# Moving three small jobs of a state-space main loop off VectorE, with new places for all small steps

## The chip, the cores and the metric

The kernel runs on one core of one Trainium2 chip. Its measure is the device time of one execution in microseconds (us), lower is better. Engines are named as in the profile: PE (TensorE matmul; PEld is its weight load), DVE (VectorE), ACT (ScalarE), POOL (GpSimd) and SP (SyncE, which here issues DMAs).

## The reference, cut to what matters

64 images are cut into 196 patches each and embedded into 192 channels; with a class token that gives 197 tokens per image. Then comes one block with a selective state-space layer, and a routed feed-forward layer with 8 experts. Cut to what the change touches:

```
def _forward(x, W_in, conv_w, conv_b, W_x, W_dt, b_dt, A_log, D, W_out, gamma, beta):
    xz = x @ W_in
    x_inner, z = jnp.split(xz, 2, axis=-1)
    x_conv = lax.conv_general_dilated(x_inner, conv_w, ...) + conv_b
    x_conv = silu(x_conv)
    BC = x_conv @ W_x
    Bm, Cm = jnp.split(BC, 2, axis=-1)
    delta = jax.nn.softplus(x_conv @ W_dt + b_dt)
    A = -jnp.exp(A_log)
    def step(h, inp):
        x_t, d_t, B_t, C_t = inp
        A_disc = jnp.exp(d_t[:, :, None] * A)
        h = A_disc * h + (d_t * x_t)[:, :, None] * B_t[:, None, :]
        y_t = jnp.einsum('bds,bs->bd', h, C_t)
        return (h, y_t)
    ...
    y = y * silu(z)
    out = y @ W_out
    mu = jnp.mean(out, axis=-1, keepdims=True)
    var = jnp.mean(jnp.square(out - mu), axis=-1, keepdims=True)
    return (out - mu) * lax.rsqrt(var + 1e-05) * gamma + beta
h = h + _L0_attn_ref(_layernorm(h, axis=-1), ...)
h = h + _L0_ffn_ref(_layernorm(h, axis=-1), ...)
```

The first layer norm is over the embedded tokens, the second ("out" norm) is the one inside the state-space layer, the third is in front of the router.

## The kernel before, in words

Images are worked on in 32 pairs; a pair is 2 x 197 = 394 columns. One body of the main loop holds several pairs at different depths: pair i is scanned, pair i+1 gets its convolution, B, C and softplus, pair i+2 its embedding and first norm, and pair i-1 its output product and its norms. Bodies run from i = -2 to 33, so that there are 32 bodies with a scan.

The scan of a pair is 12 units `u` (3 channel blocks x 4 groups of states), each in two halves, 24 half units `k`. For one unit PE spreads a row group of B over the partitions (`spread_b`, into one PSUM bank), DVE multiplies it with delta*u (`bx`, L1302), ACT makes the decays by an exponential with a scale from `neg_a` (`decays`, L661, two instructions for each half unit, into one of only two PSUM buffers), DVE scans each half unit (`scan`, L1311), POOL multiplies the states with C (`times_c`, L489) and PE sums the states (`state_sum`, L970). DVE takes the sum of a channel block times the gate into `y` (`take_y`, L1324).

Around that skeleton stand the small steps, each written at a fixed unit or half unit of the `body` function of its engine, with waits on semaphores. There is no scheduler: every engine runs its rows in the order written, and a row that waits holds all behind it. `decays(n, k)` waits until scan k-2 has ended, since the two decay buffers alternate. `kbank(K, odd)` gives the small products two PSUM banks in turn, and the numbers `K_OF`, `OUT`, `TOKS`, `FT`, `BT`, `CS`, `ROUTE` say which product has which bank; the waits in PE's `body` follow that order.

The steps that the change moves from DVE are three. `out_stats` computes the mean and variance of the output product of pair i-1 (BATCH_NORM_STATS2 L1285, BATCH_NORM_AGGREGATE L1290), after which POOL makes a reciprocal deviation and a bias (`rstd`, L478 to L483) and ACT applies both (`normalise`, L668). `softplus_t` rounds 1 + exp(-|v|) and takes the 1 away again (L1340), which POOL uses for the lost part of the logarithm. `last_bc` makes the third bf16 part of the product that holds B and C (L1317); three bf16 parts together carry an fp32 value through a bf16 matmul.

Behind the loop the tokens get their router probabilities, ranks and slots. Most columns, `FIRST` (the first 31 pairs), are treated inside the last bodies; those of the last pair, `LAST`, after them. The steps are `shift`, an exponential on ACT, `weigh` (L1360 to L1364), `choose` (L1369 to L1374), `rank` on PE and `ranks` on DVE (L1383 to L1397).

## Time and profile before

| | before |
|---|---|
| median of 3 runs | 3121.68 us (3120.38 to 3123.74) |
| the profiled execution's own time | 3125.05 us |
| its span from first to last instruction | 3123.3 us |
| mean granted clock of PE, as a share | 0.899 |
| busy over the span: PE, DVE, ACT, POOL | 2551.4, 2516.7, 1970.8, 2153.0 us |

The span is split into a start (to the first `bx` at 121.94 us), the 32 scan bodies (to 2473.55 us, the end of the last scan), the router work and the expert layer. In a row of the profile the times are microseconds from the start of the span; an idle time in brackets is the wait of the engine just before the row, with what ended it.

### The profile page before, as it was taken

Reading aid. Unit: us, or ns where it says so; the run is one execution under the profiler, and the core shown is the slowest. Engines: PE = TensorE matmul, PEld = TensorE weight load, DVE = VectorE, ACT = ScalarE, POOL = GpSimd, SP = SyncE. Lnnn points to the kernel's source line nnn. Section 1 sums busy time; section 2 is a strip of 40 time slices with the busy share of each in tenths; the row PEclk is TensorE's granted clock in tenths of the full one; section 3 lists DMA queues with packets and bytes.
Section 4 is the critical chain, followed back from the end, with each engine's and each line's share of the span. In section 5 each row is a group of like instructions: output and inputs, shape, how many; then the busy total and the mean of one; then the engine's idle time right before and its main releaser. Section 6 shows DMA issues by size and latency. Waiting matters only on the chain.

```text
span 3123.3 us, 38093 instructions
## 1 busy us (share of the span) xinstructions
PE 2551.4 (82%) x12714; PEld 1570.2 (50%) x12714; DVE 2516.7 (81%) x2800; ACT 1970.8 (63%) x3883; POOL 2153.0 (69%) x1291
## 2 busy tenths in 40 slices
PE   5688888878888888888888878788886567999997
PEld 3344444444444444444444444444442256888886
DVE  1499999999999999999999999999999875322222
ACT  0577777777777777777777777777676464333332
POOL 0378788877888887778888887788787613544442
PEclk8899899988899999989999998888898679999999
DMA  3344444444554544444444444454453023666652
GB/s 95 93 94 101 102 101 105 115 115 108 114 118 116 115 107 102 102 102 101 102 101 101 102 117 106 114 114 114 108 118 91 8 74 111 220 215 206 210 188 99
DMA packets 165466, 361.10 MB, mean 116 GB/s; under 512 B 18353, under 2 KB 89593, under 8 KB 157848
## 3 DMA queue, kind: packets, MB, share of 16 engines
q1 hardware_dynamic: 152504, 329.59, 42.0%
q0 software_dynamic: 12768, 29.08, 2.9%
q8 instruction: 103, 1.69, 0.2%
q14 instruction: 91, 0.75, 0.1%
HBM read 293.86 MB, written 69.30 MB: 116 GB/s over the span
## 4 chain that ended last, share of the span: by engine, by line
PE 38%; DVE 33%; issue 13%; ACT 13%; POOL 1%; DMA 1%; SPq 0%; DVEq 0%; POOLq 0%; ACTq 0%
DVE arena L1311 15%; DVE arena L1302 11%; PE banks L1218 7%; PE banks L1197 5%; PE banks L941 4%; PE banks L904 4%; PE banks L1205 2%; PE banks L970 2%; PE banks L932 2%; PE banks L923 2%; ACT banks L661 2%; ACT arena L668 1%; DVE arena L1340 1%; DVE arena L1285 1%; ACT L741 1%
## 5 line engine op out<-in xcount | busy, mean ns | idle before, releaser
L489 POOL TENSOR_TENSOR arena<-arena 128x1576 f32<-128x1576 f32 x384 | 1244.2, 3255 | 286.7 <-DVE arena L1311 286.7
L1311 DVE TENSOR_TENSOR_SCAN arena<-banks,arena 128x788 f32<-128x788 f32 x768 | 1359.8, 1789 | 58.7 <-ACT banks L661 20.5
L661 ACT ACTIVATE banks<-arena,neg_a 128x392 f32<-128x392 f32 x1536 | 842.3, 581 | 421.8 <-DVE arena L1311 415.2
L1302 DVE TENSOR_TENSOR arena<-arena,banks 128x1576 f32<-128x1576 f32 x384 | 681.3, 1774 | 29.4 <-DMA arena<-delta_du_scratch 16.8
L970 PE MATMUL banks<-arena,gather_q 128*32 128x394 f32 x3072 | 380.2, 571 | 0.2 <-POOL arena L489 0.2
L1513 DVE TENSOR_TENSOR arena<-banks,arena 128x384 f32<-128x384 f32 x57 | 31.8, 558 | 346.3 <-PE banks L1218 346.3
L904 PE MATMUL banks<-wtok,arena 128*99 128x192 f32 x1536 | 264.3, 329 | 49.1 <-ACT arena L728 44.3
L923 PE MATMUL banks<-arena,v_lo 128*128 128x394 f32 x768 | 291.5, 523 | 2.5 <-ACT arena L698 1.1
L904 PEld LDWEIGHTS banks<-wtok,arena 128*99 128x99 f32 x1536 | 249.0, 167 | 81.2 <-ACT arena L728 65.6
L624 POOL DMA_INDIRECT out_tokens<-arena x114 | 114.7, 1006 | 245.0 <-DVE arena L1528 225.2
L668 ACT ACTIVATE arena<-arena 99x192 f32<-99x192 f32 x384 | 178.8, 536 | 124.2 <-POOL arena L483 119.6
L1218 PE MATMUL banks<-arena 128*128 128x192 f32 x1368 | 232.5, 326 | 0.7 <-DVE arena L1513 0.7
L1218 PEld LDWEIGHTS banks<-arena 128*128 128x128 f32 x1368 | 221.5, 190 | 1.4 <-DVE arena L1513 1.0
L923 PEld LDWEIGHTS banks<-arena,v_lo 128*128 128x128 f32 x768 | 143.3, 196 | 153.8 <-issue 59.2
L914 PE MATMUL banks<-ident,arena 99*128 99x99 f32 x128 | 43.6, 366 | 216.1 <-ACT arena L698 127.3
L941 PE MATMUL banks<-arena,wdt 128*128 128x394 f32 x576 | 211.1, 512 | 5.7 <-ACT arena L737 4.9
L862 ACT ACTIVATE arena<-banks 128x256 f32<-128x256 f32 x57 | 22.0, 385 | 304.1 <-PE banks L1184 304.1
L616 POOL DMA_INDIRECT arena<-rows_scratch,arena x114 | 118.0, 1035 | 122.2 <-DVE arena L1505 87.8
L955 PE MATMUL banks<-arena,pick 128*128 128x394 bf16 x384 | 142.5, 371 | 71.5 <-DVE arena L1302 71.4
L941 PEld LDWEIGHTS banks<-arena,wdt 128*128 128x128 f32 x576 | 105.5, 192 | 113.7 <-issue 29.3
L1197 PE MATMUL banks<-arena 128*128 128x256 f32 x684 | 159.1, 381 | 4.0 <-ACT arena L864 2.4
L970 PEld LDWEIGHTS banks<-arena,gather_q 128*32 128x32 f32 x3072 | 64.2, 115 | 189.1 <-issue 184.8
(217 smaller groups left out, 4237.8 us busy)
## 6 DMA issues: line engine op xcount, KB each, us to landing
arena<-delta_du_scratch SPq DMA_DIRECT2D x384, 394.0 KB, 11.2
arena<-in_w_pack SPq DMA_DIRECT2D x57, 1155.0 KB, 5.2
delta_du_scratch<-arena SPq DMA_DIRECT2D x96, 394.0 KB, 3.3
arena<-in_x SPq DMA_DIRECT2D x32, 1176.0 KB, 15.8
rows_scratch<-arena SPq DMA_DIRECT2D x32, 297.0 KB
rows_scratch<-arena SPq DMA_DIRECT2D x32, 294.0 KB
arena<-in_b SPq DMA_DIRECT2D x57, 96.0 KB, 5.2
arena<-in_conv_w SPq DMA_DIRECT2D x1, 2304.0 KB, 9.1
```

What stands on the lines that cost most here:

```text
L489: pool.tensor_tensor(v[:, :, :], v[:, :, :], c_rep[r][:, u % NG].unsqueeze(1).to_broadcast([P, NQ, N2]), ALU.mult).then_inc(s_mulp, 1)
L661: ins = act.activation(o, d, ACT.Exp, scale=neg_a[:, c:c + 1])
L668: ins = act.activation(dst(c), src(c), ACT.Identity, scale=rs[:, c:c + 1], bias=nb[:, c:c + 1])
L904: mm = pe.matmul(v[0:H0, f * DIM:(f + 1) * DIM], patches[:, c, b, f * HSTEP:f * HSTEP + H0], wtok[:, c, :], start=(c == 0), stop=(c == KP ...
L923: pe.matmul(v[:, 0:N2], v_lo[:, k, c], t_lo[:, :, k:k + L], start=(k == 0), stop=False)
L941: mm = pe.matmul(v[:, 0:N2], wdt[:, k, c], xz[r][:, k, :], start=(k == 0), stop=(k == MB - 1))
L955: pe.matmul(ps_b[:, 0:N2], pick[:, u % NG, :], bc3[r], start=True, stop=True).then_inc(s_bb, 1)
L970: mm = pe.matmul(ps_y[q * 32:(q + 1) * 32, 0:N2], gather_q[:, :], hb[u % BUFS][:, q, :], start=False, stop=(g == NG - 1), skip_group_check ...
L1197: pe.matmul(hidden_part(k, f), wp[g][:, f * P:(f + 1) * P], x[:, 0, :], start=(f not in (2, 3, 5)), stop=False, skip_group_check=True)
L1218: mm = pe.matmul(ps_out[:, f * DIM:(f + 1) * DIM], hid[k % 2][:, c, f * P:(f + 1) * P], w2[:, c, :], start=(c == 0), stop=(c == KF - 1))
L1302: dve.tensor_tensor(hb[u % BUFS][:, :, :], rep[m][:, :, 1, :], ps_b[:, 0:N2].unsqueeze(1).to_broadcast([P, NQ, N2]), ALU.mult).then_inc(s_ ...
L1311: dve.tensor_tensor_scan(v, decay[k % 2], v, 0.0, ALU.mult, ALU.add).then_inc(s_scan, 1)
```

## The change

Three jobs leave DVE, and all small steps of all four engines get new units, half units and banks.

The output norm: the columns of `wout` are centred once in the start (the mean of each row is taken away), so that the product has a mean of zero; ACT then squares the product with `Square` and an accumulated sum (`out_squares`), POOL makes the reciprocal deviation from it in two instructions instead of four (`rstd_out`), and ACT applies it as a scale alone. The softplus rounding becomes two ACT instructions, +1 and -1 (`softplus_up`, `softplus_t`). The third part of B and C becomes a subtraction on POOL (`last_bc`) and a copy to bf16 on ACT (`third_bc`).

The places: the third norm's application, the back transposes and the router of a pair run one body later than before (pair i-2 instead of i-1), two of the three convolutions and the copy of the gate's `Silu` run one body earlier, two of the four C spreads one body later, and at the end `choose` and `ranks` of `FIRST` stand behind the loop instead of inside it.

```diff
-        K_OF = (0, 1, 2, 6, 5, 7, 8, 9, 14, 13)
-        MADE = (1, 2, 3, 5, 4, 6, 7, 8, 10, 9)
-        TAKEN = (1, 3, 2, 5, 4, 6, 7, 8, 10, 9)
-        OUT, TOKS, FT = (3, 4), (10, 11), (16, 18)
-        BT, CS, ROUTE = (19, 20), (12, 15, 17, 21), 22
+        K_OF = (21, 1, 20, 4, 5, 9, 8, 13, 16, 14)
+        MADE = (2, 3, 1, 4, 5, 7, 6, 8, 10, 9)
+        TAKEN = (2, 3, 1, 4, 5, 7, 6, 8, 10, 9)
+        OUT, TOKS, FT = (6, 7), (11, 12), (17, 18)
+        BT, CS, ROUTE = (3, 10), (19, 22, 0, 2), 15
...
+            def rstd_out(n):
+                need(pool, s_onorm, n)
+                pool.wait_ge(s_sq2, n + 1)
+                pool.tensor_scalar(var2[:, :], sq2[:, :], 1.0 / DIM, EPS, ALU.mult, ALU.add).then_inc(s_var2, 1)
+                pool.wait_ge(s_var2, n + 1)
+                pool.tensor_tensor(rs2[:, :], var2[:, :], small[0:H0, 0, :], ALU.pow).then_inc(s_rs2, 1)
...
+            def last_bc(n, r):
+                pool.wait_ge(s_bcmid, n + 1)
+                pool.tensor_tensor(bcf, bcf, bc3[r], ALU.subtract).then_inc(s_bclast, 1)
...
+            def out_squares(n, r):
+                act.wait_ge(s_oev, 2 * (n + 1))
...
+                for c in range(4):
+                    ins = act.activation(rows[r][:, c, DIM:2 * DIM], ob[:, c, :], ACT.Square, accum_out=sq2[:, c:c + 1])
+                ins.then_inc(s_sq2, 1)
+
             def out_norm(n):
-                normalise(n, lambda c: ob[:, c, :], lambda c: ob[:, c, :], rs2, nb2, s_rs2, s_onorm, range(4))
+                act.wait_ge(s_rs2, n + 1)
+                for c in range(4):
+                    ins = act.activation(ob[:, c, :], ob[:, c, :], ACT.Copy, scale=rs2[:, c:c + 1])
+                ins.then_inc(s_onorm, 1)
...
+            def third_bc(n, r):
+                act.wait_ge(s_bclast, n + 1)
+                act.activation(bc3[r][P - 2 * NS:P], bcf[P - 2 * NS:P], ACT.Copy).then_inc(s_bc3, 1)
...
+            def softplus_up(n):
+                act.wait_ge(s_spe, n + 1)
+                need(act, s_ddu, DDU * n)
+                act.activation(delta[:, :, :], spe[:, :, :], ACT.Identity, bias=1.0).then_inc(s_spu, 1)
+
+            def softplus_t(n):
+                act.wait_ge(s_spu, n + 1)
+                act.activation(delta[:, :, :], delta[:, :, :], ACT.Identity, bias=-1.0).then_inc(s_spt, 1)
...
-            def last_bc(n, r):
-
-                v = slice(P - 2 * NS, P)
-                dve.wait_ge(s_bcmid, n + 1)
-                dve.tensor_tensor(bc3[r][v], bcf[v], bc3[r][v], ALU.subtract).then_inc(s_bc3, 1)
-
...
-            def out_stats(n):
-                stats(n, lambda c: ob[:, c, :], st2, mv2, s_oev, 2 * (n + 1), s_rs2, s_st2, s_mv2)
-
...
-            def softplus_t(n):
-                dve.wait_ge(s_spe, n + 1)
-                need(dve, s_ddu, DDU * n)
-                dve.tensor_scalar(delta[:, :, :], spe[:, :, :], 1.0, -1.0, ALU.add, ALU.add).then_inc(s_spt, 1)
...
-                    if -1 in on and k == 10:
-                        out_stats(i - 1)
-                        if i == PAIRS:
-                            choose(FIRST)
...
-                    if 1 in on and k == 15:
-                        last_bc(i + 1, o)
-                    if 1 in on and k == 15:
-                        softplus_t(i + 1)
...
+                    if -2 in on and k == 19:
+                        take_logits(i - 2, r)
+                        if i == PAIRS:
+                            shift(FIRST)
+                        if i == PAIRS + 1:
+                            weigh(FIRST, 1)
...
             for i in range(-2, PAIRS + 2):
                 body(i, i % 2, range(-i, PAIRS - i))
+            choose(FIRST)
+            ranks(FIRST, 1)
```

DVE, half units 10 to 15 of one middle body. L1302 is `bx`, L1311 the scan (listed under this name by the compiler), L1285 and L1290 the statistics, L1317 `last_bc`, L1340 `softplus_t`, L1277 the embedding, L1324 `take_y`. Before:

```order
L1311 SCALAR_TENSOR_TENSOR arena<-banks,arena 128x788
L1285 BN_STATS arena<-arena 99x6 x4
L1290 BN_AGGR arena<-arena 99x2 x4
L1311 SCALAR_TENSOR_TENSOR arena<-banks,arena 128x788
L1302 TENSOR_TENSOR arena<-arena,banks 128x1576
L1311 SCALAR_TENSOR_TENSOR arena<-banks,arena 128x788 x2
L1302 TENSOR_TENSOR arena<-arena,banks 128x1576
L1311 SCALAR_TENSOR_TENSOR arena<-banks,arena 128x788
L1324 TENSOR_TENSOR arena<-arena,banks 128x394
L1311 SCALAR_TENSOR_TENSOR arena<-banks,arena 128x788
L1317 TENSOR_TENSOR arena<-arena 32x394
L1340 TENSOR_SCALAR arena<-arena 128x3x394
```

The same stretch in the changed kernel, half units 10 to 16, where L1386 is `bx`, L1395 the scan, L1402 `take_y` and L1361 the embedding:

```order
L1386 TENSOR_TENSOR arena<-arena,banks 128x1576
L1395 SCALAR_TENSOR_TENSOR arena<-banks,arena 128x788 x2
L1386 TENSOR_TENSOR arena<-arena,banks 128x1576
L1395 SCALAR_TENSOR_TENSOR arena<-banks,arena 128x788 x2
L1402 TENSOR_TENSOR arena<-arena,banks 128x394
L1386 TENSOR_TENSOR arena<-arena,banks 128x1576
L1395 SCALAR_TENSOR_TENSOR arena<-banks,arena 128x788
L1361 TENSOR_TENSOR arena<-banks,tok_bias 99x384
L1395 SCALAR_TENSOR_TENSOR arena<-banks,arena 128x788
L1386 TENSOR_TENSOR arena<-arena,banks 128x1576
L1395 SCALAR_TENSOR_TENSOR arena<-banks,arena 128x788
L1361 TENSOR_TENSOR arena<-banks,tok_bias 99x384
```

The eight rows of the output statistics and the rows L1317 and L1340 are gone; `take_y` and the embedding stand a half unit earlier.

ACT, half units 9 and 10. Before, with L741 the `Silu` of z, L737 that of x and L680 the copy of the output product:

```order
L661 ACTIVATE banks<-arena,neg_a 128x2x196 x2
L741 ACT_TABLE_LOAD
L741 ACTIVATE arena<-arena 128x1182
L737 ACTIVATE arena<-arena 128x1182
L680 ACTIVATE arena<-banks 99x384
L661 ACT_TABLE_LOAD
L661 ACTIVATE banks<-arena,neg_a 128x2x196 x2
L680 ACTIVATE arena<-banks 99x384
```

The changed kernel, half units 9 to 13, with L680 the decays, L699 the copies of the output product, L708 the squares, L754/L755 the softplus reads, L780 the exponential, L785 and L789 +1 and -1, L801/L802 a copied back transpose:

```order
L699 ACTIVATE arena<-banks 99x384 x2
L708 ACTIVATE arena<-arena 99x192 x4
L680 ACTIVATE banks<-arena,neg_a 128x2x196 x4
L754 ACTIVATE arena<-banks,bdt 128x394
L755 ACTIVATE arena<-banks,bdt 128x394
L680 ACTIVATE banks<-arena,neg_a 128x2x196 x2
L754 ACTIVATE arena<-banks,bdt 128x394
L755 ACTIVATE arena<-banks,bdt 128x394
L780 ACTIVATE arena<-arena 128x1182
L680 ACTIVATE banks<-arena,neg_a 128x2x196 x2
L785 ACTIVATE arena<-arena 128x3x394
```

The two `Silu` instructions, which shared one pair of table loads, now stand apart (L776 at the end of a body, L772 in half unit 5), each with a load ahead of it and one behind it:

```order
L776 ACT_TABLE_LOAD
L776 ACTIVATE arena<-arena 128x1182
L680 ACT_TABLE_LOAD
L680 ACTIVATE banks<-arena,neg_a 128x2x196 x2
```

```order
L772 ACT_TABLE_LOAD
L772 ACTIVATE arena<-arena 128x1182
L734 ACTIVATE arena<-banks 128x394
L801 ACTIVATE arena<-banks 128x198
L802 ACTIVATE arena<-banks 64x198
L680 ACT_TABLE_LOAD
L680 ACTIVATE banks<-arena,neg_a 128x2x196 x2
```

So a body has six table loads on ACT, where it had four.

## Rows read from the trace of the kernel before

**Rows 1.** Busy time of each engine in a middle stretch.

```profile
core 0: us, PE busy (x) PEld busy (x) DVE busy (x) ACT busy (x) POOL busy (x), PEclk, DMA share, GB/s
1500.00:2000.00 500.00, 411.81 (x1989) 222.71 (x1991) 482.65 (x465) 360.41 (x675) 404.35 (x216) 0.90 0.48 111
```

**Rows 2.** What DVE waited for, 500 to 2300 us: total, times, longest.

```profile
DVE arena L1311 <- ACT banks L661: 16.8, 25, 1.2
DVE arena L1302 <- PE banks L955: 7.8, 8, 2.0
```

**Rows 3.** Timeline of DVE: start, duration, row, count, idle before.

```profile
165.81 0.77 DVE L1317 TENSOR_TENSOR arena<-arena 32x394 bf16<-32x394 f32 x1
...
1530.91 1.77 DVE L1302 TENSOR_TENSOR arena<-arena,banks 128x1576 f32<-128x1576 f32 x1
...
1536.19 1.77 DVE L1302 TENSOR_TENSOR arena<-arena,banks 128x1576 f32<-128x1576 f32 x1
...
1551.28 1.11 DVE L1285 BATCH_NORM_STATS2 arena<-arena 99x6 f32<-99x192 f32 x4
1552.85 0.38 DVE L1290 BATCH_NORM_AGGREGATE arena<-arena 99x2 f32<-99x6 f32 x4 [0.46 <-DVE arena L1285]
1553.14 1.76 DVE L1311 TENSOR_TENSOR_SCAN arena<-banks,arena 128x788 f32<-128x788 f32 x1
...
1565.97 0.74 DVE L1317 TENSOR_TENSOR arena<-arena 32x394 bf16<-32x394 f32 x1
...
1568.05 0.55 DVE L1277 TENSOR_TENSOR arena<-banks,tok_bias 99x384 f32<-99x384 f32 x1
```

**Rows 4.** Groups of ACT by form, 1500 to 2260 us.

```profile
L661 ACT ACTIVATE banks<-arena,neg_a 128x392 f32<-128x392 f32 x495 | 271.5, 581 | 125.6 <-DVE arena L1311 124.8
L668 ACT ACTIVATE arena<-arena 99x192 f32<-99x192 f32 x128 | 59.6, 536 | 20.8 <-POOL arena L483 19.3
L661 ACT ACT_TABLE_LOAD x21 | 26.9, 1283 | 0.4
...
L737 ACT ACTIVATE arena<-arena 128x1182 f32<-128x1182 f32 x10 | 11.8, 1176 | 0.0
```

**Rows 5.** Timeline of ACT around one table load.

```profile
1542.06 1.10 ACT L661 ACTIVATE banks<-arena,neg_a 128x392 f32<-128x392 f32 x2 [0.49 <-DVE arena L1311]
1543.18 1.28 ACT L741 ACT_TABLE_LOAD   x1
1544.47 1.19 ACT L741 ACTIVATE arena<-arena 128x1182 f32<-128x1182 f32 x1
```

**Rows 6.** Groups of POOL by form, 1500 to 2260 us.

```profile
L489 POOL TENSOR_TENSOR arena<-arena 128x1576 f32<-128x1576 f32 x123 | 398.6, 3257 | 80.9 <-DVE arena L1311 80.9
...
L495 POOL TENSOR_TENSOR arena<-arena 128x394 f32<-128x394 f32 x10 | 9.3, 934 | 10.2 <-ACT arena L718 10.2
```

**Rows 7.** Timeline of PE: one softplus product early, and one in the middle.

```profile
148.43 4.02 PE L941 MATMUL banks<-arena,wdt 128*128 128x394 f32 x6 [1.13 <-ACT arena L737]
...
1547.17 2.25 PE L941 MATMUL banks<-arena,wdt 128*128 128x394 f32 x6
```

**Rows 8.** Timeline of DVE, POOL and PE behind the last scan.

```profile
2471.76 1.79 DVE L1311 TENSOR_TENSOR_SCAN arena<-banks,arena 128x788 f32<-128x788 f32 x1
...
2482.46 0.57 DVE L1324 TENSOR_TENSOR arena<-arena,banks 128x394 f32<-128x394 f32 x1 [0.61 <-PE banks L970]
...
2518.97 0.17 DVE L1445 TENSOR_SCALAR arena<-arena 99x8 int32<-99x8 f32 x1
...
2467.94 12.86 POOL L489 TENSOR_TENSOR arena<-arena 128x1576 f32<-128x1576 f32 x4
...
2510.40 0.48 PE L999 MATMUL banks<-sww_hi,arena 128*99 128x8 f32 x2
```

**Rows 9.** Busy time of each engine in two stretches: `weigh`, and `choose` to `ranks`.

```profile
2482.93:2486.52 3.59, 3.35 (x11) 3.08 (x12) 3.51 (x5) 0.00 (x0) 0.00 (x0) 0.50 0.00 0
2491.24:2512.35 21.11, 10.45 (x32) 5.54 (x32) 15.38 (x29) 4.71 (x12) 15.66 (x27) 0.64 0.10 30
```

More of the change, by code:

```diff
@@ L594, in body @@
                             router_consts()
-                    if 0 in on and u == 5:
+                    if 0 in on and u == 2:
                         fill_rows(i, r)
-                    if -1 in on and u == 8:
+                    if -1 in on and u == 7:
                         apply_gamma(i - 1)
+                    if 2 in on and u == 7:
+                        rstd(i + 2, 1)
                     if -1 in on and u == 8:
@@ new lines, in body @@
+                    if 0 in on and k == 2:
+                        copy_c(i, r, r, 2)
+                    if -2 in on and k == 2:
+                        row_norm(i - 2, r)
+                        if i == PAIRS + 1:
+                            router_exp(FIRST, 1)
+                    if 1 in on and k == 4:
+                        copy_product(i + 1, o, r, 1)
+                    if 1 in on and k == 5:
+                        silu_x(i + 1, o)
+                    if 0 in on and k == 5:
+                        copy_c(i, r, r, 3)
@@ L1114, in body @@
-                    if -1 in on and u == 10:
+                        if 2 in on:
+                            pe.wait_ge(s_trf_copied, 2 * (i + 2) + 1)
+                        else:
+                            pe.wait_ge(s_lg, i - 2 + 1)
+                        spread_c(i + 1, o, r, 0)
+                    if 2 in on and u == 10:
+                        pe.wait_ge(s_trf_copied, 2 * (i + 2) + 2)
+                        conv(i + 2, r, r, 2)
+                    if 2 in on and u == 11:
                         if 1 in on:
-                            pe.wait_ge(s_cc, NG * (i + 1) + 3)
+                            pe.wait_ge(s_cc, NG * (i + 1) + 1)
@@ L1143, in _ @@
                 body(i, i % 2, range(-i, PAIRS - i))
+            rank(FIRST, 1)
             rank(LAST, 2)
```

283 lines of the change are left out of this document (152 added, 131 removed).

## The prediction

> **What bounds the kernel now.** I read the busy times of a middle stretch first. DVE is busy 482.7 of 500 us (97%), POOL 404, ACT 360 and PE 412 [rows 1]. Then the waits of DVE: from 500 to 2300 us, some 24.5 bodies, its two main rows lost 16.8 + 7.8 us; with the few small entries of the same answer it is 27.4 us, which is 1.12 us per body [rows 2]. So the loop runs at the pace of DVE's own instruction list. The reader is to see that nothing but the length of that list and these short waits sets the time of a body. From one `last_bc` at 165.81 to the one nineteen bodies later at 1565.97 is 1400.2 us, 73.69 us for one body [rows 3]. The list alone is 73.69 - 1.12 = 72.57 us. A unit (one `bx`, two scans) takes 5.28 us of it [rows 3].
>
> **What leaves DVE.** The output statistics take 1.86 us from their start to the next scan, with 0.46 us of idle reported where a gap of about 0.1 stands in other groups, so 1.52 us of work [rows 3]. `last_bc` and `softplus_t` take 2.08 us from start to the next row, and about 0.07 us of wait stands ahead of them: 2.15 us [rows 3]. Together 3.67 us per body; the list becomes 68.9 us. Only an equal set of rows stays, so nothing else of DVE changes its price.
>
> **What it costs the others, per body.** ACT gets four squares. The nearest row is the same shape with two operands by partition, 0.536 us, about 1.8 us for four overlapping ones; the accumulated sum appears nowhere in the trace. I take 1.8, with ends of 1.4 and 2.8. Further +1 and -1 at 1.18 us each, like L737, about 0.5 us for the copy of the third part, and two table loads of 1.28 us [rows 4]. That is 7.2 us. Summed over its own rows from start to start ACT then has about 59 us of a body, where it had 52: under 68.9. POOL gets a subtraction of 0.93 us and loses two small ones of the four in `rstd`, and stays near 60 us, of which twelve `times_c` of 3.26 us are 39 [rows 1, 6]. PE's products are unchanged, 412/500 x 73.69 = 61 us per body [rows 1]. No engine is above the 68.9 us in sum. Nothing in SP's queue is added; `store_rows` comes half a body later, and the load of delta for the third channel block behind it still has over 30 us before its scans.
>
> **Whether the new places hide it.** Sums don't tell this, because only two decay buffers stand between ACT and DVE. From the end of scan k-2 ACT has, for an even k, 5.3 us until the decays of k+1 must be ready, and for an odd k 7.1 us (two units' worth less one scan); two pairs of decays take 2.1 us of it, so 3.2 or 5.0 us are left for extras. I walked ACT, PE, POOL and DVE once round a body with the starts from these rows. The tight places:
> - Half unit 5, `Silu` of x with two loads, a C copy and a back transpose: 4.5 us. ACT came in late from the third norm in half unit 2; about 0.9 us to spare.
> - Half unit 9, both output copies and the squares, behind the output product that PE must first finish: 0.6 us to spare, the least of all.
> - Half units 12 and 13, exponential, +1, -1: about 1.0 us. Half unit 15, logarithm and two loads: 1.3 us. End of the body, `Silu` of z with two loads: 1.3 us.
> - POOL's chain from `softplus_sum` to `make_du` is followed by one `times_c`, gamma and the first norm's deviation, on which ACT's `front_norm` waits: 1.9 to 2.5 us to spare, and the same before the row statistics.
> - PE in unit 7 has an embedding product and two z products ahead of the spread of B for unit 9: 1.1 to 1.4 us.
> All of it closes, but by little, and PE's products were taken at the length of the middle row, 2.25 us for six matmuls; after an idle stretch the same six took 4.02 us, at the lower of the clock's two levels, 1.2 against 2.4 GHz [rows 7]. Such dips will now and then use up a margin of 1 us, as they did before (waits on L955 of up to 2.0 us [rows 2]). On the other side the old wait of 0.7 us per body on ACT lay where both `Silu` stood, and that crowd is gone. I take 0.6 us of waits per body, where it was 1.12, with ends of 0 and 2.2. A body is 68.9 + 0.6 = 69.5 us, 4.19 us less.
>
> **The end of the loop.** Here the change loses. `choose` and `ranks` of `FIRST` ran while the last pair's norms went round POOL and ACT. Now `weigh` follows the last pair's logits, and the rest follows it. Behind the last scan, which ends at 2473.55, the last `take_y` began 8.9 us later, because POOL had waited on a norm before four late `times_c`; the logits product ended 37.3 us later, and L1445, where the common work begins, came at 45.4 us [rows 8]. In the new order POOL has only one `times_c` left, so `take_y` starts about 4 us sooner and the logits are there at some 33 us. But then come `weigh`, 3.6 us, and `choose`, PE's ranks and `ranks`, 21.1 us, in a row [rows 9]; and the same steps for `LAST`, 6.6 us from 2512.35 to L1445. That is 64.3 us, 19 us later than before. Ends: 15 and 23 us.
>
> **The start.** The first `bx` waits for the delta of pair 0. On POOL and ACT the chain to it is as long as before: +1 and -1 run beside `softplus_sum`. The three `wout` rows on DVE lie ahead of the first embedding, where DVE waited for PE. I take 0.
>
> **Sum.** 31 of the scan bodies hold the removed rows and the change in waits: 31 x 4.19 = 130, less 19, is 111 us. The profiled execution took 3125.05 us, its span 3123.3, so it would take about 3014; it lies 3.4 us above the median of the runs, so I predict 3121.7 - 111 = 3010.7, rounded to 3011 us. From here the measurement could tell no change within 0.2%, 6 us.
>
> **Rivals.**
> - DVE stays the bound with waits of 0 to 1.6 us per body (my forecast): 31 x 4.79 - 15 = 133 us at best, so 2988; 31 x 3.19 - 19 = 80 us at worst, so 3042. Chance 0.72.
> - A wait takes the place of some that went: ACT late at half units 5 and 9, or PE late with the spread of B in unit 9, by 1.6 to 4 us per body. For it speaks that ACT stands at 59 of 69 us with buffers for one half unit, against it that every margin of the walk is positive. At 2.5 us: 31 x 2.29 - 19 = 52, 3070. Chance 0.16.
> - Slower: a table load holds ACT twice its row. Six loads, three pairs of them, in half units 5, 15 and the last, would each pair be 2.6 us later against margins of 0.9, 1.3 and 1.3 us, 4.3 us of waits per body on top of 0.6. The point from which waits decide is 4.79 - 19/31 = 4.2 us; at 4.9 us it is 31 x 0.11 + 19 = 22 us slower, 3144. The trace speaks against it: the row before the load ends at 1543.16, the load runs from 1543.18, and the next row starts at 1544.47 [rows 5]. With every other way to 4.2 us or more I give 0.09.
> - The gain is there but the end of the loop and waits eat it, within 6 us of before: waits of 4.0 to 4.4 us. Chance 0.03.
>
> The Trainium skill, page "ScalarE: Activation LUTs", section "What ACT_TABLE_LOAD costs", gives a switch 1283 ns for the load and some 1380 ns more for a drain, 2.66 us in all. By that rule the time would be that of the third rival, about 3144; the loads of the trace are 1283 ns each and show no drain beside them, so by the rows the rule's second half does not hold here. Its section "Rules for kernel authors" has additions go to VectorE and not ScalarE, which is against moving the rounding; that holds for the sum of busy time (2.4 us on ACT for 1.4 on DVE), not for the engine that sets the pace.
>
> **Range and chances.** The forecast's own cases reach from 2988 to 3042. To leave out no more than 2 in 10 I go to 3062 above, which takes in half of the second rival, and stay at 2988 below. Faster by over 0.2%: 0.72 + 0.16 = 0.88; within it 0.03; slower 0.09.
>
> **What would show it.** One `bx` to the same one a body later should be 69.5 us apart (68.9 if all is hidden). DVE's waits on L680, the decays, and L1007, the spread of B, should sum to under 1 us per body; if half unit 10 or 6 shows waits on the decays, the squares or the `Silu` are too long for their place. The row L708 should be near 0.5 us. ACT should show six loads of 1.28 us per body with no gap behind. Between the last scan and the row that was L1445 there should be 64 us, with DVE idle for some 8 us ahead of the last logits. The prediction fails if a small wait recurs in most bodies: each us per body is 31 us.

## The result and the profile after

| | median, us | range, us |
|---|---|---|
| before, same chip | 3122.71 | 3120.38 to 3125.78 |
| changed | 3026.93 | 3025.51 to 3027.41 |

The ratio is 0.9697, 95% interval 0.9685 to 0.971: 96 us less, against 111 predicted. The time lies in the range (2988 to 3062) and the forecast case came about. The page of the changed kernel, its middle stretch and the waits of DVE from 500 to 2200 us (total, times, longest) answer to [rows 1, 2]:

```profile
span 3025.3 us, 38157 instructions
...
1500.00:2000.00 500.00, 439.95 (x2103) 243.51 (x2102) 481.75 (x422) 420.57 (x798) 428.22 (x225) 0.91 0.49 115
...
DVE arena L1395 <- ACT banks L680: 27.6, 40, 1.1
DVE arena L1395 <- DVE arena L1386: 1.4, 3, 0.5
```

DVE is as full as it was (481.8 of 500 us), with fewer rows for a body. ACT rose to 420.6, POOL to 428.2. Both DVE rows are scans (L1395, before L1311); the first waits for the decays (L680, before L661). The embedding's first half (L1361) marks a body. It stands here 25 bodies apart:

```profile
443.49 0.53 DVE L1361 TENSOR_TENSOR arena<-banks,tok_bias 99x384 f32<-99x384 f32 x1
...
2194.56 0.53 DVE L1361 TENSOR_TENSOR arena<-banks,tok_bias 99x384 f32<-99x384 f32 x1
```

That is 1751.07 / 25 = 70.04 us for one body. The waits are 29.0 us in 1700 us, 24.3 bodies: 1.19 us per body. So DVE's list is 68.85 us. Half units are counted from 0, as `k` in the kernel. Two places make nearly all of the waits: 24 waits stand ahead of the scan of half unit 7, 17.9 us in all, and 13 ahead of that of half unit 10, 8.3 us. In the timelines of DVE, ACT and PE of one body (start, duration, row, count, idle before it), both waits are to be seen:

```profile
1532.81 0.30 PE L1043 MATMUL banks<-ident,arena 99*128 99x99 f32 x1 [1.23 <-ACT arena L743]
...
1534.55 0.34 PE L1007 MATMUL banks<-arena,pick 128*128 128x394 bf16 x1 [1.18 <-DVE arena L1386]
...
1536.88 4.31 PE L984 MATMUL banks<-arena,wx 128*128 128x394 f32 x6 [1.10 <-ACT arena L734]
...
1541.23 0.50 ACT L748 ACTIVATE arena<-banks 128x394 f32<-128x394 f32 x1 [1.56 <-PE banks L984]
...
1542.00 1.10 ACT L680 ACTIVATE banks<-arena,neg_a 128x392 f32<-128x392 f32 x2
...
1543.14 1.80 DVE L1395 TENSOR_TENSOR_SCAN arena<-banks,arena 128x788 f32<-128x788 f32 x1 [0.99 <-ACT banks L680]
...
1549.52 0.49 ACT L699 ACTIVATE arena<-banks 99x384 f32<-99x384 f32 x1 [1.46 <-PE banks L1034]
...
1552.56 3.49 DVE L1395 TENSOR_TENSOR_SCAN arena<-banks,arena 128x788 f32<-128x788 f32 x2 [0.66 <-ACT banks L680]
```

Read it backwards from 1543.14, the scan of half unit 7. The scan waits for decays that ACT starts at 1542.00, behind the copies of B and C (L748 and L749, next to it). Those waited 1.56 us for PE's product of B and C (L984), six matmuls that took 4.31 us. Ahead of them PE had three gaps of 1.23, 1.18 and 1.10 us within 5.3 us, with short products between. The windows of the same stretch have the granted clock in the third column from the end:

```profile
1531.00:1534.00 3.00, 1.14 (x9) 0.44 (x5) 3.00 (x3) 2.75 (x6) 1.12 (x1) 1.00 0.90 242
1534.00:1535.47 1.47, 0.92 (x9) 0.25 (x9) 1.37 (x2) 1.46 (x2) 1.47 (x1) 1.00 1.07 327
1535.47:1536.88 1.41, 0.30 (x4) 0.00 (x1) 1.41 (x2) 1.41 (x3) 1.41 (x2) 0.50 1.12 292
1536.88:1541.00 4.12, 4.12 (x7) 2.20 (x8) 4.02 (x4) 2.76 (x5) 1.03 (x1) 0.50 1.06 177
```

PE was busy 1.14 of 3.00 us and then 0.92 of 1.47 us, with two of the gaps in them. At 1535.47, before the third gap began, the granted clock fell to 0.50, the lower level (1.2 of 2.4 GHz), and the whole product ran at that. The group of the B and C product from 500 to 2200 us, here (L984) and before (L932):

```profile
L984 PE MATMUL banks<-arena,wx 128*128 128x394 f32 x144 | 97.6, 847 | 25.7 <-ACT arena L734 25.7
L932 PE MATMUL banks<-arena,wx 128*128 128x394 f32 x138 | 51.8, 511 | 12.8 <-ACT arena L680 12.8
```

Before, the six took 2.25 us in every body of that stretch. Here 12 of the 24 products took 4.31 us and the other 12 took 3.67 to 4.04, because the clock was back at 1.00 before they ended. The second wait, 0.66 us at 1552.56, is that of half unit 10. It stands behind the squares of half unit 9, which stand behind the output product (L1034) and its copies (L699). All 13 waits of this kind stand in bodies whose B and C product took 4.31 us.

Behind the last scan (DVE, answering to [rows 8]):

```profile
2353.88 3.49 DVE L1395 TENSOR_TENSOR_SCAN arena<-banks,arena 128x788 f32<-128x788 f32 x2
...
2361.67 0.57 DVE L1402 TENSOR_TENSOR arena<-arena,banks 128x394 f32<-128x394 f32 x1 [4.31 <-PE banks L1022]
...
2389.98 0.19 DVE L1409 TENSOR_TENSOR logits<-banks,swb 99x32 f32<-99x32 f32 x1 [9.10 <-PE banks L1052]
...
2420.95 0.17 DVE L1507 TENSOR_SCALAR arena<-arena 99x8 int32<-99x8 f32 x1
```

The last scan ends at 2357.37; L1507, which was L1445, starts 63.6 us later, where it was 45.4. So the sum reads: first `bx` at 122.19 (before 121.94), 0.25 us lost; from there to the end of the last scan 2235.2 us (before 2351.6), 116.4 us gained; the end of the loop, 18.2 us lost; behind it 604.4 us (before 604.3). That is 98 us, the difference of the two spans (3123.3 and 3025.3).

The new rows of ACT (groups by form, 1500 to 2200 us, ten bodies):

```profile
L680 ACT ACT_TABLE_LOAD x30 | 38.5, 1283 | 5.4 <-DVE arena L1395 5.0
L714 ACT ACTIVATE arena<-arena 99x192 f32<-99x192 f32 x41 | 15.2, 440 | 0.0
L708 ACT ACTIVATE arena<-arena 99x192 f32<-99x192 f32 x40 | 14.0, 351 | 0.3
...
L708 ACT ACTIVATION_READ_ACCUMULATOR arena<-arena 99x1 f32 x40 | 7.5, 187 | 0.0
```

### The profile page after: what moved, and what is told of

Its sections match the earlier page's. It is cut to its first block, busy times and chain, and to the rows that moved or that the text cites. A ratio compares the mean times of both kernels' runs of the same rounds, so it can differ in the third digit from the quotient of the medians.

```text
span 3025.3 us, 38157 instructions
## 1 busy us (share of the span) xinstructions
PE 2577.4 (85%) x12714; PEld 1602.4 (53%) x12714; DVE 2400.3 (79%) x2483; ACT 2158.4 (71%) x4296; POOL 2162.7 (71%) x1259
## 3 DMA queue, kind: packets, MB, share of 16 engines
q8 instruction: 103, 1.69, 0.2%
## 4 chain that ended last, share of the span: by engine, by line
DVE 37%; PE 34%; ACT 15%; issue 12%; POOL 1%; DMA 1%; SPq 0%; DVEq 0%; POOLq 0%; ACTq 0%
DVE arena L1395 18%; DVE arena L1386 13%; PE banks L1296 7%; PE banks L1275 5%; ACT banks L680 4%; PE banks L984 4%; PE banks L956 3%; PE banks L1283 3%; PE banks L1034 3%; PE banks L993 3%; DVE arena L1369 2%; PE banks L1022 2%; ACT L772 1%; ACT arena L772 1%; ACT arena L708 1%
## 5 line engine op out<-in xcount | busy, mean ns | idle before, releaser
L1395 DVE TENSOR_TENSOR_SCAN arena<-banks,arena 128x788 f32<-128x788 f32 x768 | 1350.9, 1787 | 75.3 <-ACT banks L680 36.8
L680 ACT ACTIVATE banks<-arena,neg_a 128x392 f32<-128x392 f32 x1536 | 834.9, 580 | 144.1 <-DVE arena L1395 134.5
L1386 DVE TENSOR_TENSOR arena<-arena,banks 128x1576 f32<-128x1576 f32 x384 | 681.9, 1776 | 17.3 <-DMA arena<-delta_du_scratch 17.1
L1022 PE MATMUL banks<-arena,gather_q 128*32 128x394 f32 x3072 | 373.3, 561 | 1.5 <-POOL arena L502 1.5
L956 PEld LDWEIGHTS banks<-wtok,arena 128*99 128x99 f32 x1536 | 277.6, 187 | 62.5 <-issue 52.8
L956 PE MATMUL banks<-wtok,arena 128*99 128x192 f32 x1536 | 305.3, 362 | 6.0 <-DVE skip L1348 4.8
L1007 PE MATMUL banks<-arena,pick 128*128 128x394 bf16 x384 | 133.9, 349 | 187.4 <-DVE arena L1386 187.4
L687 ACT ACTIVATE arena<-arena 99x192 f32<-99x192 f32 x256 | 118.8, 536 | 147.8 <-POOL arena L496 147.8
L1007 PEld LDWEIGHTS banks<-arena,pick 128*128 128x128 bf16 x384 | 37.4, 97 | 259.9 <-DVE arena L1386 190.7
L993 PEld LDWEIGHTS banks<-arena,wdt 128*128 128x128 f32 x576 | 115.5, 205 | 105.8 <-issue 25.4
L984 PE MATMUL banks<-arena,wx 128*128 128x394 f32 x192 | 129.8, 845 | 37.6 <-ACT arena L734 34.3
```

Source lines behind the costliest of these rows:

```text
L680: ins = act.activation(o, d, ACT.Exp, scale=neg_a[:, c:c + 1])
L956: mm = pe.matmul(v[0:H0, f * DIM:(f + 1) * DIM], patches[:, c, b, f * HSTEP:f * HSTEP + H0], wtok[:, c, :], start=(c == 0), stop=(c == KP ...
L984: mm = pe.matmul(v[:, 0:N2], wx[:, k].rearrange("p c n -> p (c n)"), xz[r][:, k, :], start=(k == 0), stop=(k == MB - 1))
L993: mm = pe.matmul(v[:, 0:N2], wdt[:, k, c], xz[r][:, k, :], start=(k == 0), stop=(k == MB - 1))
L1007: pe.matmul(ps_b[:, 0:N2], pick[:, u % NG, :], bc3[r], start=True, stop=True).then_inc(s_bb, 1)
L1022: mm = pe.matmul(ps_y[q * 32:(q + 1) * 32, 0:N2], gather_q[:, :], hb[u % BUFS][:, q, :], start=False, stop=(g == NG - 1), skip_group_check ...
```

## The experiments

Theory: a body is as long as DVE's list plus DVE's waits, and what is left of the waits comes from PE's low clock ahead of half unit 7 (some of the expectations below call it the eighth) and from the squares in half unit 9. Rivals: ACT's own load of 59 us per body makes the waits; or the new places and not the moved work earned the gain.

The runs were made on two chips. The kernel before took 3120.57 us (7 runs) beside the first four and 3138.74 to 3140.94 us beside the other eight. In the traces of all eight the extra time stands behind the row that is L1507 in the changed kernel, 621 to 625 us where the first chip has 604. So I compare differences to the kernel before that ran beside each; the body of before is from the first chip's trace. "Body" is measured as above, from one first embedding row to one 21 to 25 bodies later; "waits" are all waits of DVE from 500 to 2200 us, for one body; "list" is body less waits.

| kernel | ratio, 95% interval | to before, us | body, us | waits, us | list, us |
|---|---|---|---|---|---|
| before | 1 | 0 | 73.64 | 1.10 | 72.53 |
| changed | 0.9697 (0.9685, 0.971) | -95.8 | 70.04 | 1.19 | 68.85 |
| `tail_back` | 0.9664 (0.9648, 0.968) | -104.8 | 69.96 | 1.11 | 68.85 |
| `c3_early` | 0.9693 (0.9677, 0.9709) | -96.3 | 70.00 | 1.14 | 68.86 |
| `squares_10` | 0.9675 (0.9659, 0.9692) | -102.1 | 69.96 | 1.05 | 68.92 |
| `pe_fill` | 0.959 (0.9574, 0.9606) | -128.7 | 68.94 | 0.14 | 68.80 |
| `un_stats` | 0.9834 (0.9813, 0.9854) | -52.8 | 71.64 | 1.10 | 70.54 |
| `un_round` | 0.9853 (0.9833, 0.9873) | -47.4 | 71.68 | 1.59 | 70.09 |
| `un_third` | 0.9789 (0.9769, 0.9809) | -67.8 | 71.11 | 1.53 | 69.59 |
| `places_only` | 1.0014 (1.0005, 1.0024) | +3.7 | 73.38 | 0.97 | 72.42 |
| `old_places` | 1.0427 (1.0406, 1.0449) | +134.2 | 78.51 | 9.29 | 69.22 |
| `old_round_back` | 1.0075 (1.0059, 1.009) | +24.8 | 74.85 | 4.53 | 70.32 |
| `fill_other` | 0.9701 (0.9686, 0.9715) | -94.3 | 69.96 | 1.12 | 68.84 |
| `c3_fill_sq10_tail` | 0.9553 (0.954, 0.9566) | -139.7 | 68.93 | 0.14 | 68.79 |

### The waits that are left

**`pe_fill`.** Twenty constant products per body, 118 columns of the unit matrix each, go into columns of y's bank that nothing reads: seven ahead of the back transposes in unit 1, seven and six round the spread of B in unit 2, where PE stood idle. In the rows each such product is two matmuls.

```diff
+            def filler(count):
+                for _ in range(count):
+                    pe.matmul(ps_y[:, N2:512], ident[:, :], ident[:, 0:512 - N2], start=False, stop=False,
+                              skip_group_check=True)
...
                 for u in range(UNITS):
+                    if 1 in on and -1 in on and u == 2:
+                        filler(7)
                     if 0 in on and u + 1 < UNITS:
                         spread_b(i, r, u + 1)
+                    if 1 in on and -1 in on and u == 2:
+                        filler(6)
...
+                    if 1 in on and -1 in on and u == 1:
+                        filler(7)
                     if -2 in on and u == 1:
```

> The changed kernel with 20 small fp32 products of two constants (118 columns each, into columns of the PSUM bank of y that nothing reads) in the three gaps of PE ahead of the B/C product. They add work to PE and take nothing away. My theory (the B/C product takes 4.3 us in place of 2.2 because TensorE's clock fell in these gaps): the granted clock there stays at the high level, the six matmuls take 2.2 us, the wait of DVE behind them (1.0 us per body) goes and with it part of the wait behind the squares (0.2 to 0.6 us): 20 to 40 us faster, about 2997 us. Rival (waits come from ACT's own 59 us of work): 3027 us or slower, since 20 matmuls of more PE work stand ahead.

PE's timeline there (the first and the last of the three groups of products), the window of the B and C product, and DVE's waits from 500 to 2200 us:

```profile
1508.43 1.72 PE L1040 MATMUL banks<-ident 128*128 128x118 f32 x14
...
1512.08 1.49 PE L1040 MATMUL banks<-ident 128*128 128x118 f32 x12
...
1514.29 2.25 PE L984 MATMUL banks<-arena,wx 128*128 128x394 f32 x6
...
1514.29:1516.50 2.21, 2.21 (x11) 1.36 (x8) 2.21 (x3) 2.19 (x3) 0.67 (x1) 1.00 1.07 178
...
DVE arena L1406 <- DVE arena L1397: 1.8, 4, 0.5
DVE arena L1406 <- ACT banks L680: 0.9, 2, 0.5
```

The six products take 2.25 us at full clock, and the waits for the decays fall from 27.6 us to 0.9. The product even starts later than in the changed kernel, 4.56 us behind the start of its unit's `bx` where it was 4.16, so it is its length and not its start that counts. A body is 1.10 us shorter; the kernel gains 33 us on the changed one. Work that computes nothing made it faster. ACT does all that it did, so its own load isn't the cause, which drops the first rival; the squares of half unit 9 fit too once the chain ahead of them is on time.

**`fill_other`.** Fourteen such products in other gaps: seven ahead of the spread in unit 6, three in unit 9, four in unit 10.

```diff
+            OTHER = {6: 7, 9: 3, 10: 4}
...
+                    if 1 in on and -1 in on and u in OTHER:
+                        filler(OTHER[u])
```

> The changed kernel with 14 of the same constant products per body, in other gaps of PE (7 ahead of spread_b in unit 6, 3 in unit 9, 4 in unit 10), and none ahead of the B and C product. It tells the place of the filling from its amount. My theory: the six products of B and C stay at about 0.86 us each, VectorE's waits stay at 1.1 us per body, and the time is that of the changed kernel within 5 us (ratio 0.968 to 0.972). Rival (any filling helps, since the engine's clock is one over the whole body): six products near 0.5 us, a ratio of 0.962 or less.

```profile
1500.00:2000.00 500.00, 447.04 (x2311) 257.93 (x2310) 481.56 (x421) 420.79 (x800) 428.65 (x225) 0.95 0.49 115
...
L984 PE MATMUL banks<-arena,wx 128*128 128x394 f32 x144 | 97.3, 844 | 25.9 <-ACT arena L734 25.9
...
DVE arena L1404 <- ACT banks L680: 25.9, 39, 1.0
```

The middle stretch and, from 500 to 2200 us, the group of the B and C product and DVE's main wait. The mean clock rose from 0.91 to 0.95, but a matmul of B and C still takes 844 ns, and the time is the changed kernel's within 1.5 us. The mean clock by itself is worth nothing here; the clock under one product, on which ACT and then DVE wait, is worth 33 us.

**`c3_early`.** The fourth copy of C, whose bank the B and C product reuses, goes ahead of the `Silu`.

```diff
+                    if 0 in on and k == 4:
+                        copy_c(i, r, r, 3)
                     if 1 in on and k == 5:
                         silu_x(i + 1, o)
-                    if 0 in on and k == 5:
-                        copy_c(i, r, r, 3)
```

> The changed kernel with one ACT row moved: the copy of the fourth C spread from half unit 5, behind the Silu of x, to half unit 4. It frees the bank of the B/C product. My theory: the B/C product then starts when Silu ends, 0.4 us sooner, but still at the low level of TensorE's clock, so the wait of DVE behind its copy shrinks from about 1.0 to 0.6 us per body: 31 x 0.4 = 12 us faster, 3015 us. Rival (ACT's amount of work sets the waits, not where the product starts): within 3 us of 3027 us.

A miss: no gain beyond the interval. The product now waits for the `Silu` and not for the copy, but that brings it forward by only 0.1 us: it starts 4.06 us behind its unit's `bx` (1532.23 to 1536.29), where it was 4.16 (1532.72 to 1536.88). The copy in front makes the `Silu` itself 0.2 us later. The matmuls take 845 ns as before, and the waits for decays are 26.3 us where they were 27.6. So this run doesn't tell what an earlier start would be worth, since it hardly made one.

**`squares_10`.** The squares go one half unit later (`k == 9` to `k == 10`).

> The changed kernel with one ACT job moved: the four squares from half unit 9 to half unit 10, so that one pair of decays goes ahead of them. My theory: the wait of DVE before the tenth half unit's scan (about 0.2 to 0.6 us per body) goes, the other wait stays at 1.0: 5 to 15 us faster, 3017 us. Rival (the wait only moves to the next pair of decays): within 3 us of 3027 us.

```profile
DVE arena L1395 <- ACT banks L680: 23.1, 25, 1.0
DVE arena L1395 <- DVE arena L1386: 2.3, 5, 0.5
```

DVE's waits for the decays from 500 to 2200 us: 25 where there were 40, now one per body, at half unit 7 (0.94 us). The 8.3 us at half unit 10 are gone, but those at half unit 7 rose from 17.9 to 22.6, since the B and C product was at the lower clock for longer: 882 ns for a matmul where it was 847. The kernel is 6 us faster than the changed one, with intervals that still overlap. A body gains only 0.08 us, 2.5 us in 31 bodies; 3.4 us more lie in an earlier first `bx` (121.04) and a shorter end (61.3 us). So the squares held the second wait, but it followed from the first: it stood only in bodies with a product of 4.31 us, and `pe_fill`, with the squares where they were, has none of it.

### The end of the loop

**`tail_back`.** The exponent of `FIRST` goes into half unit 19 of body 32 (`i == PAIRS`, the last but one), `weigh` and `choose` into the wait for the last pair's logits, `ranks(FIRST, 1)` behind `weigh` of `LAST`.

```diff
...
                     if -1 in on and k == 20:
                         row_stats(i - 1, o)
+                        if i == PAIRS:
+                            weigh(FIRST, 1)
+                            choose(FIRST)
...
-            choose(FIRST)
-            ranks(FIRST, 1)
-
-
             shift(LAST)
             weigh(LAST, 2)
+            ranks(FIRST, 1)
```

> The changed kernel with the router work of FIRST moved back into the last bodies: its exponential, weigh and choose in body 32 behind the row statistics, shift and weigh of LAST ahead of ranks(FIRST). The loop is untouched. My theory (the end of the loop lost 18 us because weigh, choose, the rank products and ranks of FIRST run in a row behind the last logits): the time from the last scan to the row after ranks(LAST) goes from 63.6 to some 53 us, so 10 to 12 us faster than the changed kernel, about 3016 us. Rival (the last pair's norms are what is long there, and the order of the router work is hidden): within 2 us of the changed kernel, 3027 us.

```profile
2354.62 3.49 DVE L1395 TENSOR_TENSOR_SCAN arena<-banks,arena 128x788 f32<-128x788 f32 x2
...
2381.55 1.15 DVE L1430 TENSOR_REDUCE arena<-arena 99x124 f32<-99x992 f32 x1
...
2390.98 0.18 DVE L1409 TENSOR_TENSOR logits<-banks,swb 99x32 f32<-99x32 f32 x1
...
2410.58 0.17 DVE L1505 TENSOR_SCALAR arena<-arena 99x8 int32<-99x8 f32 x1
```

`weigh` and `choose` (2381.55 to 2391) now fill the wait of 9.10 us ahead of the last logits. From the end of the last scan, 2358.11, to L1505 it is 52.5 us instead of 63.6. The kernel is 9 us faster than the changed one; the 11 us of the end are seen whole in the trace. Seven us of the 18 stay: the ranks of `FIRST` still follow the last logits, where in the kernel before they ran ahead of them.

### The work and the places

**`un_stats`, `un_round`, `un_third`.** Each gives one job back to VectorE, all other places as in the changed kernel: the statistics at half unit 11 (squares and the two-step deviation gone), the rounding at 12 (+1 and -1 on ACT gone), the last part of B and C at 10 (the POOL and ACT rows gone).

```diff
-                    if -1 in on and k == 9:
-                        out_squares(i - 1, o)
+                    if -1 in on and k == 11:
+                        out_stats(i - 1)
```

```diff
-                    if 1 in on and k == 13:
-                        softplus_up(i + 1)
...
-                    if 1 in on and k == 13:
-                        softplus_t(i + 1)
+                    if 1 in on and k == 12:
+                        softplus_t(i + 1)
```

```diff
-                    if 1 in on and k == 18:
-                        third_bc(i + 1, o)
+                    if 1 in on and k == 10:
+                        last_bc_dve(i + 1, o)
```

> The changed kernel, with the second normalisation's statistics back on VectorE, at half unit 11, and ScalarE's squares gone. My theory (VectorE's list sets the body; its waits come on top): the list grows by the 1.52 us of bn_stats and bn_aggr in the trace of before, 31 x 1.52 = 47 us; the wait of about 0.6 us before half unit 10, which stood behind the squares, should go, 31 x 0.6 = 19 us. So about +28 us against the changed kernel, 3055 us, with 3075 if no wait goes. Rival (ScalarE's length sets the body, 1.4 us of squares less): no slower than the changed kernel.

> The changed kernel, with the softplus rounding back on VectorE as one instruction at half unit 12, and ScalarE's two instructions gone. My theory: the list grows by the 1.31 us or so of that instruction, 31 x 1.31 = 41 us, and no wait goes, since the waits stand at half units 8 and 10 and the two ScalarE rows at 13: about 3068 us. Rival (ScalarE's relief takes waits away too): 3040 us or less.

> The changed kernel, with the last part of B's and C's third piece back on VectorE at half unit 10, and the POOL and ScalarE rows that took its place gone. My theory: the list grows by about 0.8 us, 31 x 0.8 = 25 us, and the waits stay: about 3052 us. Rival (POOL's chain was late and its relief gives something back): under 3040 us.

They cost 43, 48 and 28 us against the changed kernel. The list grows by 1.69, 1.24 and 0.74 us where 1.52, 1.31 and 0.8 were expected: the terms of the list hold to 0.2 us. The waits didn't do what I wrote. With the squares gone, the wait at half unit 10 went, but one of 0.5 us per body on the embedding product came (11.2 us in 23), so `un_stats` has 1.10 us of waits, as before. In the other two, ACT was relieved and the waits rose to 1.59 and 1.53 us. Less work on ACT bought nothing. What changed with the waits is the clock under the B and C product: from 500 to 2200 us one of its matmuls takes 891 ns in `un_round`, where all 23 products took 4.31 us, and 869 in `un_third`, against 847 in the changed kernel. That the clock alone made these waits longer was not tested; neither kernel was run with constant products.

**`places_only`.** All three jobs back on VectorE, all new places kept.

> All three jobs back on VectorE, everything else at the changed kernel's places. My theory (each job costs its place in VectorE's list, and the places alone earn nothing in a body): the three single returns measured 0.0137, 0.0156 and 0.0092 of the time against the changed kernel's ratio, 0.0385 together, so a ratio of about 1.008, 18 us of it the end of the loop: about 3147 us. Rival (the new places alone make the body shorter): a ratio of 0.995 or less.

The ratio is 1.0014: 3.7 us slower than before, where the sum of the three single returns was 1.008. The single returns cost 119 us together, but two of them also raised the waits, by 0.40 and 0.34 us per body; with all three the waits are 0.97 us. The list is 72.42 us (before 72.53). A body is 0.26 us shorter, some 8 us in 31, and the end of the loop takes 61.3 us where it took 45.4, which is 16 more. The places alone earn nothing. They bring the lower clock, though: a matmul of B and C takes 870 ns here with VectorE's work as before, and 511 in `old_places`.

**`old_places`.** The kernel before with the three jobs taken off VectorE and every other step where it was: squares at half unit 11, rounding and third part on ACT at half unit 16, `last_bc` in POOL's unit 7.

```diff
+                    if -1 in on and k == 11:
+                        out_squares(i - 1, o)
...
+                    if 1 in on and k == 16:
+                        softplus_up(i + 1)
+                    if 1 in on and k == 16:
+                        third_bc(i + 1, o)
+                    if 1 in on and k == 16:
+                        softplus_t(i + 1)
...
-                        out_stats(i - 1)
...
-                    if 1 in on and k == 15:
-                        last_bc(i + 1, o)
-                    if 1 in on and k == 15:
-                        softplus_t(i + 1)
```

> The kernel before with all its small steps at their old places, and only the three jobs taken off VectorE (squares at half unit 11, the rounding and the third piece on ScalarE at half unit 16, the last part on POOL at unit 7, the output weights centred). It tells the moved places from the moved work. My theory: the list is 3.67 us shorter than before, 31 x 3.67 = 114 us; the waits of before (1.12 us per body) grow, since ScalarE gets 7 us per body more at places that were not cleared for it, by 0 to 2.5 us per body (0 to 78 us); the loss of 18 us behind the last scan should not come, since the tail's steps stand where they stood. So 3010 to 3085 us, about 3035. Rival (the new places earned nothing): 3008 us, 18 us below the changed kernel.

By far the largest miss: 134 us slower than before, 230 slower than the changed kernel, with a list as short as predicted (69.2 us). DVE's waits from 500 to 2200 us, and ACT, PE and DVE at the largest of them:

```profile
DVE arena L1338 <- PE banks L958: 122.5, 21, 5.9
DVE arena L1363 <- PE banks L1009: 42.5, 44, 1.8
DVE arena L1372 <- ACT banks L682: 34.0, 44, 1.2
...
1575.19 1.19 ACT L787 ACTIVATE arena<-arena 128x1182 f32<-128x1182 f32 x1
1576.40 0.53 ACT L770 ACTIVATE arena<-arena 32x394 bf16<-32x394 f32 x1
1576.95 1.19 ACT L791 ACTIVATE arena<-arena 128x1182 f32<-128x1182 f32 x1
...
1579.07 0.47 ACT L761 ACTIVATE arena<-banks 128x394 f32<-128x394 f32 x1
...
1579.60 5.57 PE L958 MATMUL banks<-wtok,arena 128*99 128x192 f32 x24 [3.04 <-ACT arena L761]
...
1585.21 0.56 DVE L1338 TENSOR_TENSOR arena<-banks,tok_bias 99x384 f32<-99x384 f32 x1 [5.85 <-PE banks L958]
```

+1, the third part and -1 (L787, L770, L791) stand ahead of a copy of the gate's product (L761), whose bank PE needs for the second embedding product (L958). PE waits 3.04 us, in which the granted clock falls to 0.50 (at 1579.12), then takes 5.57 us for a product that takes 4.14 at full clock, and DVE stands still for 5.85 us.

**`old_round_back`.** The same, with the rounding back on VectorE at half unit 15 and its two ACT rows gone.

> The kernel with the old places and the three jobs off VectorE (ratio 1.043), but with the softplus rounding back on VectorE at half unit 15. My theory: the wait of 5.85 us before the second embed row is ScalarE's crowd at half units 16 and 17, in which two rounding instructions of 1.19 us stand ahead of the copy that PE waits for; with both gone the wait falls by about 2.2 us and the list grows by 1.3 us: a ratio of 1.03 to 1.035. Rival (the wait comes from the squares and the output's chain instead): the wait stays near 5.9 us and the time grows by 40 us, a ratio of 1.055.

```profile
DVE arena L1359 <- PE banks L1005: 42.7, 40, 2.0
DVE arena L1368 <- ACT banks L682: 34.7, 47, 1.2
DVE arena L1334 <- PE banks L954: 24.3, 23, 1.1
...
1578.75 0.50 ACT L761 ACTIVATE arena<-banks 128x394 f32<-128x394 f32 x1
...
1579.30 4.14 PE L954 MATMUL banks<-wtok,arena 128*99 128x192 f32 x24 [0.96 <-ACT arena L761]
```

Right in kind, too small in size. The wait before the second embedding row falls from 5.85 to some 1.06 us, by 4.8 and not by 2.2. The copy L761 starts 0.47 us behind the first embedding row's start (1578.28), where it was 3.85 (1575.22 to 1579.07). Of these 3.4 us, 2.4 are the two ACT rows; the rest goes with VectorE's own rounding, 1.36 us at 1577.01, which now stands ahead of the first embedding row. The other 1.4 us are the product, 4.14 us for 5.57: PE waited 0.96 us ahead of it and not 3.04, and the granted clock stayed at 1.00. The list grows by 1.1 us, and the kernel gains 109 us. The other two rows, 42.7 us on the spread of B (L1005) and 34.7 us on the decays, stay, and so does most of what these places still cost.

### All that helped

**`c3_fill_sq10_tail`** has the edits of `pe_fill`, `c3_early`, `squares_10` and `tail_back`.

> All that helped in one kernel: the constant products ahead of the B and C product, the fourth copy of C before the Silu, the squares one half unit later, and the router's exponent, weights and choice moved into the last bodies. My theory: the list of 68.85 us is untouched, the waits are near nothing already with the products alone (0.9 us in 1700 us), so only the end of the loop adds to them: 11 us less than the kernel with the products, a ratio of about 0.955, 2981 us against 3121.68. Rival (the two small moves still earn 3 to 8 us): a ratio of 0.953 or less.

```profile
DVE arena L1406 <- DVE arena L1397: 1.8, 4, 0.5
DVE arena L1406 <- ACT banks L680: 0.9, 2, 0.5
```

The ratio is 0.9553: 140 us less than before, 44 less than the changed kernel, 11 less than `pe_fill`, which is the end of the loop (52.3 us) and no more. A body is DVE's list of 68.8 us with 0.14 us of waits. The two small moves earn nothing beside the products. This is the fastest kernel of the study.

## Why the prediction was right, and where its sizes were off

- **What leaves DVE: right.** Predicted 3.67 us and a list of 68.9 us; the list is 68.85, and with all three jobs given back 72.42, 3.57 us more.
- **The waits: the term that was mis-sized.** Predicted 0.6 us per body, measured 1.19, so a body of 70.04 instead of 69.5. Over 31 bodies that is 18 us less than forecast. The loop gained 116.4 us where 130 was the forecast, 13.6 less: 31 x 3.60 is 112, and some 5 us came back in bodies outside the stretch in which I measured. The old waits did go, as predicted (from 500 to 2200 us 15.0 us on the decays of half unit 10, behind the two `Silu`, and 7.7 us on the spread of B); new ones took their place. The step that failed is the one that took PE's products at 2.25 us and the low clock as something that comes "now and then". It comes under the B and C product of every body from 500 to 2200 us (mean 847 ns where 511 stood), since the new places leave PE three gaps right ahead of it; `places_only` has the same with 870 ns. `pe_fill` shows the cause: full clock under that product, no waits. `fill_other` shows that a higher clock in other stretches earns nothing. The trace of before had held the price (4.02 against 2.25 us [rows 7]), but the walk round a body looked at the length of PE's gaps only as spare time.
- **The tight places: half right.** Half unit 9, "the least of all", did show a wait, 0.66 us, which goes when the squares move. The larger wait, at half unit 7, wasn't in the list: its chain is `Silu`, fourth C copy, B and C product, copy of it, decays. The prediction took waits at half unit 10 or 6 as a sign that the squares or the `Silu` "are too long for their place": at 10 they appeared although the squares were shorter than estimated, 1.4 us from 1550.05 to 1551.44 with their reads, for 1.8; what stood ahead of them was late. One bracket in the walk is off: "two units' worth less one scan" would be 8.8 us; the 7.1 us used are two units less two scans, which is the right figure.
- **The other engines: right.** ACT 420.57/500 x 70.04 = 58.9 us (59 predicted; by the same measure before has 53.1 and not 52, so 5.8 us were added and not 7.2, with the squares at 1.4 us for 1.8 and the output norm's application 0.1 us cheaper for each of its four), POOL 60.0 (near 60), PE 61.6 (61). No engine took the bound from DVE.
- **The end of the loop: right.** 63.6 us for 64.3, 18.2 us lost for 19; the last logits 32.6 us behind the last scan for some 33. `tail_back` shows that 11 us of it are the placing of `weigh` and `choose`.
- **The start: right**, 0.25 us for 0.
- **The rival with the table loads: rejected.** Six loads per body stand at 1283 ns each, and behind each of the 60 loads in ten bodies the next row starts within 0.02 us; the load of L776 runs from 1588.11 for 1.28 us and its `Silu` starts at 1589.40. The Trainium skill, page "ScalarE: Activation LUTs", section "What ACT_TABLE_LOAD costs", adds a drain of some 1380 ns for a switch; the trace of the changed kernel doesn't show it.
- **The rival with waits of 1.6 to 4 us: not here, but near.** `un_round` and `un_third` come to its edge (1.59 and 1.53 us), and `old_places` (9.3 us) and `old_round_back` (4.5 us), with the moved work at other places, go beyond it. The prediction's 0.16 for it rested on a walk with margins of 0.6 to 1.4 us; that the walk closed for these places was what made the change a gain. Neither half alone is one: the places alone +3.7 us, the work alone, where I put it, +134 us, both together -96. What other places for the work would have given in the old order was not tried.

## What to carry to other kernels

Where one engine's list sets the pace, price what leaves the list from its rows, and trust that; then ask of each place that gets new work which bank or buffer the next row in that queue frees, and who waits for it, since two rows of 1.2 us in the wrong place, with the lower clock that followed from them, made 109 us of the time here. When walking the chain, take TensorE's products at the lower clock wherever short gaps stand close ahead of them; if such a product lies on the chain, constant products in the gaps can be worth more than any move. A long serial piece of end work belongs in the last waits of the loop, not behind them.

## What the runs showed of the hardware that was not expected

- Two gaps of 1.23 and 1.18 us, with PE busy 1.14 of 3.00 us and then 0.92 of 1.47, stood ahead of a fall of the granted clock from 1.00 to 0.50 at 1535.47; a third gap, of 1.10 us, began after it. A single gap of 1.49 us in the kernel before, from 1538.9 to 1540.37, left the clock at 1.00. The Trainium skill, page "TensorE: Matmul & The Clock Gate", section "What's actually happening", says that the clock goes by how busy the engine has been recently; these rows agree, and no long stop was needed.
- An `ACTIVATE` with an accumulated sum brings a row of its own, `ACTIVATION_READ_ACCUMULATOR`, 187 ns, behind each of the four squares. They overlap in part: four pairs take 1.4 us.
- A `Copy` with a scale by partition took 440 ns (L714) where the application with scale and bias of the same shape took 536 ns [rows 4].
